# Recurrent mixer on one core: another order of each engine's work, joins over filled rows, weights loaded one stage earlier

## The chip, the core and the metric

The kernel runs on one core of a Trainium2 chip. A core has five engines that run their own instruction streams and meet at semaphores: TensorE (PE in the profile; its weight loads are PEld), VectorE (DVE), ScalarE (ACT), GpSimd (POOL) and SyncE (SP), whose queue here issues nearly all DMAs. The metric is the device time of one execution in microseconds, the median of several runs.

## The reference

A model of two layers over 32 samples of 114 tokens with 256 features each. The change touches the first layer's attention, a gated delta-rule recurrence, cut here to its core:

```python
mixed = hidden_states @ W_qkv.T                 # 2048 channels
y = conv_general_dilated(mixed.T, conv_w, ...)  # 4 taps, one channel each
q, k, v = split(silu(y).T, ...)                 # 8 heads of q, k; 16 of v; 64 wide
z = hidden_states @ W_z.T
beta = sigmoid(hidden_states @ W_b.T)
g = -exp(A_log) * softplus(hidden_states @ W_a.T + dt_bias)
def step(S, (q_t, k_t, v_t, g_t, b_t)):
    S = S * exp(g_t)
    delta = (v_t - k_t @ S) * b_t
    S = S + k_t[:, None] * delta[None, :]
    return S, q_t @ S
o = scan(step, 0, ...)
h = o * silu(z);  h = h * rsqrt(mean(h * h) + EPS) * norm_weight
return h @ W_out.T
```

The rest (image and text embedding, a text layer ahead of it; a mixture of experts, a state-space mixer and a last feed-forward layer behind it) is the same before and after.

## The kernel before

The kernel is a row of stages. Two matter here: `prepare` (lines 837 to 993) and `delta_net` (line 1019 on), which calls it and then runs the mixer.

`prepare` takes the samples in 8 groups of 4: a group is loaded (L864), normalised on VectorE with a power on GpSimd, turned on TensorE (L973), copied by ScalarE (L954) and stored to `xts` (L881); TensorE also makes the gates' products (L983), which VectorE reads into `gates`. SyncE's queue issues the loads and stores; ScalarE's copy of group g waits for the store of group g - 2.

`delta_net` solves the recurrence for 16 pairs of samples. For a pair it computes the projections (`project`, L1601) into `raw`, the conv (`first_tap` on ScalarE, three further taps in `conv` on VectorE, L1322), SiLU by a tanh; the decays exp(sum of g) (`decays` L1589 on TensorE, `decay_terms` and `decay_exp` on ScalarE); the products of keys with keys and queries (`products`); from them `nt`, the weights of the triangular system (L1287, VectorE), and `qd`, the masked queries with decay (`query_decay`, L1187, GpSimd). The system of 114 unknowns for 16 heads and 2 samples is solved through the inverses of its 32 x 32 diagonal blocks: `nt` goes to memory by blocks (L1108), comes back as `ue` with one block in each of the 128 partitions (L1152), is masked on GpSimd (`mask_blocks`, L1206) and inverted by 30 elimination steps of two instructions on VectorE (`eliminate`, L1248 and L1250). The inverses go to memory as they are (`ut` comes back from there, L1139) and turned (`turn_inverse` L1260; they come back into `x`, L1133). Then, for four chains (2 samples, 2 halves of the heads): `join` (L1665) and `inverse` (L1678) make two inverses of 32 into one of 64, `solve` substitutes in two halves (L1700) with a carry between them (L1690) and makes the outputs (L1707). They are multiplied by the gate (`gated`, L1335), normalised, turned and multiplied by `w_out` (L1634).

The work is a software pipeline written out by hand. One call of `iteration(p)` on each engine is one turn: the a-part (decays, products, weights) of pair p, the z-part (elimination, gate, joins, substitution) of pair p - 1, the d-part (norm, output, residual) of pair p - 2 and the projection and conv of pair p + 1. The order of the calls in `iteration` is the order of that engine's stream; nothing else sets it. Five first turns, ten turns in a loop of two, four last turns.

The joins multiply over all 114 rows: the rows of `x` between the blocks must be zero, for which GpSimd clears `x` (`clear_x`, L1196; SyncE waits for it) and VectorE clears a gap after the joins (L1272). The mixer's weights are loaded at its start on SyncE's queue (L1166), VectorE scales `taps` and `w_z` and makes `qmask`, and all engines wait for that.

Of the kernel before, what the change touches and what calls it, by code (L numbers as in the profile page):

```python
# [836 lines left out]
def prepare(c, hid, xts, gates):  # L837
# [5 lines left out]
    with ExitStack() as ctx:  # L843
        def sb(name, shape, dt=F32):
# [9 lines left out]
        (gw_in, gvar_ready, grstd_ready, gxn_ready, g_t, gxT_ready, ab_mm, ab_read, abs_done, log1p_done, g_dve, g_act) = (  # L854
            c.sem(n) for n in ("gw_in", "gvar_ready", "grstd_ready", "gxn_ready", "g_t", "gxT_ready", "ab_mm",
                               "ab_read", "abs_done", "log1p_done", "g_dve", "g_act"))
        h_in = [c.sem(f"g_h_in{n}") for n in range(HB)]
        xT_out = [c.sem(f"g_xT_out{n}") for n in range(2)]
        with nc.Block() as block:

            @block.sync
            def _(sp):
                def load(g):
                    sp.dma_start(hs[g % HB][:, :, :], hid[g * GS:(g + 1) * GS].rearrange("b s d -> s b d")).then_inc(h_in[g % HB], 16)  # L864

# [10 lines left out]
                for g in range(GROUPS):  # L876
                    if g + HB < GROUPS:
                        sp.wait_ge(gxn_ready, g + 1)
                        load(g + HB)
                    sp.wait_ge(gxT_ready, g + 1)  # L880
                    sp.dma_start(xts[:, :, g * L:(g + 1) * L], xT[g % 2][:, :, :]).then_inc(xT_out[g % 2], 16)  # L881
                for n in range(2):
                    sp.wait_ge(xT_out[n], 16 * (GROUPS // 2))

# [7 lines left out]
            def _(dve):  # L892
# [24 lines left out]
                def gate_read(g):  # L917
                    ab = ps[0:S, 4 + g % 2, 0:GS * 2 * H].rearrange("p (s h) -> p s h", s=GS)
# [6 lines left out]
                dve.wait_ge(gw_in, 64)  # L925
                for g in range(GROUPS):
                    if g + 1 < GROUPS:
                        stat(g + 1)
                    scale(g)
                    if g >= 2:  # L930
                        gate_read(g - 2)
                gate_read(GROUPS - 2)
                gate_read(GROUPS - 1)

                dve.wait_ge(ab_read, 2 * GROUPS)
# [28 lines left out]
            def _(pe):  # L964
                pe.wait_ge(gw_in, 64)

# [10 lines left out]
                def gate(g):  # L977
                    pe.wait_ge(gxT_ready, g + 1)
# [36 lines left out]
def delta_net(c, hid, xts):  # L1015
# [14 lines left out]
    with ExitStack() as ctx:  # L1030
        def sb(name, shape, dt=F32):
# [3 lines left out]
        c.stage(prepare, hid, xts, gates)  # L1035
        w_qkv, w_z, w_out = sb("w_qkv", [128, KD, 2048]), sb("w_z", [128, KD, 1024]), sb("w_out", [128, 8, D])
        taps, gain, qmask = sb("taps", [128, CT, TAPS]), sb("gain", [128, 1]), sb("qmask", [S, S])
        xT, xz = sb("d_xT", [128, KD, W]), sb("d_xz", [128, KD, W])
# [14 lines left out]
        (dw_in, d_init, xT_in, xz_in, nd_zero, nd_out, ue_in, ud_out, ut_in, qkv_mm, raw_r, tap_r, conv_r, th_r, yy_r,  # L1053
         kq_mm, qm_r, gl_r, dec_mm, e_r, nt_r, qd_r, sel_r, elim_r, z_mm, thz_r, sz_r, vt_mm, p_mm, rc_r, t_mm, xc_r,
         o_mm, og_r, osq_r, ms_r, rms_r, on_r, ot_mm, oT_r, wo_mm, h_r, d_dve, pe_gate, pool_gate, sp_gate, x_clear,
         uet_r, vd_out, u_in, zz_mm, zs_r, ww_mm, wr_r, x_gap) = (
            c.sem("d_" + s) for s in (
                "w_in", "init", "xT_in", "xz_in", "blocks_zeroed", "blocks_out", "blocks_in", "inverse_out", "inverse_in",
# [3 lines left out]
                "ms_ready", "rms_ready", "on_ready", "ot_mm", "oT_ready", "wo_mm", "h_ready", "dve", "pe_gate", "pool_gate", "sp_gate", "x_cleared",  # L1062
                "inverse_turned", "turned_out", "turned_in", "join1_mm", "join1_ready", "join2_mm", "join2_ready", "x_gap_cleared"))
        h_in = [c.sem(f"d_h_in{s}") for s in range(2)]
        h_out = [c.sem(f"d_h_out{s}") for s in range(2)]
        DW = 7
# [20 lines left out]
        with nc.Block() as block:  # L1087

            @block.sync
            def _(sp):  # L1090
# [19 lines left out]
                def iteration(p, a=True, proj=True, z=True, d=True):  # L1110
# [10 lines left out]
                    if z:  # L1121
# [7 lines left out]
                        sp.wait_ge(x_clear, r.n * 2 + 2)  # L1129
# [23 lines left out]

                sp.dma_start(nd.rearrange("s h q j i -> (s h q) (j i)").rearrange("p (a d) -> p a d", d=D),
                             c.zero_row[:, :].unsqueeze(1).to_broadcast([128, 4, D])).then_inc(nd_zero, 16)
                load_x(Pair(0, 0))
                for dst, src in (
                    (w_qkv[:, :, :], dr["L0_attn_W_qkv_t"].rearrange("(k p) n -> p k n", p=128)),
                    (taps[:, :, :], dr["L0_attn_conv_w_c"]),
                    (w_z[:, :, :], dr["L0_attn_W_z_t"].rearrange("(k p) n -> p k n", p=128)),  # L1160
                    (gain[0:DH, :], dr["L0_attn_norm_weight"].unsqueeze(1)),
                    (gain[DH:128, :], dr["L0_attn_norm_weight"].unsqueeze(1)),
                    (w_out[:, 0:4, :], dr["L0_attn_W_out_t"].rearrange("(k p) n -> p k n", p=128)[:, 0:4, :]),
                    (w_out[:, 4:8, :], dr["L0_attn_W_out_t"].rearrange("(k p) n -> p k n", p=128)[:, 4:8, :]),
                ):
                    sp.dma_start(dst, src).then_inc(dw_in, 16)  # L1166
# [11 lines left out]
            def _(pool):  # L1178
# [13 lines left out]
                def clear_x(r, s):  # L1192

                    need(pool, o_mm, r.n * 4 - 2 + 2 * s)
                    pool.sem_inc(pool_gate, 1)
                    pool.memset(x[s][:, :, :], 0.0).then_inc(x_clear, 1)  # L1196

# [15 lines left out]
                def iteration(p, a=True, proj=True, z=True, d=True):  # L1213
                    r = p.shift(-2)
                    for v in range(4):
                        if a:
                            query_decay(p, 2 * v)
                            query_decay(p, 2 * v + 1)
                        if d and v == 0:
                            gate_power(r, 0)  # L1220
                            gate_power(r, 1)
                        if z and v == 0:
                            clear_x(p.shift(-1), 0)
                            clear_x(p.shift(-1), 1)
                    if a:
# [1790 lines left out]
```

## Time and profile before

| what | value |
|---|---|
| median of 3 runs | 3087.56 us (3084.33 to 3089.98) |
| profiled execution | 3085.63 us |
| its span, first to last instruction | 3083.9 us |
| mean granted TensorE clock | 0.881 |

How to read the page: busy time of each engine, then the span in 40 slices of 77.1 us with the busy share of each slice in tenths (9 is 90% or more).

```profile
PE 2436.0 (79%) x19286; PEld 1864.6 (60%) x19286; DVE 2084.8 (68%) x5004; ACT 1244.2 (40%) x2990; POOL 815.8 (26%) x644
## 2 busy tenths in 40 slices
PE   7888887997458888888888888876452847889698
PEld 5666665886446666666666666655341735566454
DVE  4777774333368888888888888855563336876663
ACT  1334342221256566666666666642000213344132
POOL 2111100001033232232222333221377036450110
PEclk9999998997579999999999999988665877899799
```

`prepare` runs from 739 to 802 us, the mixer from there to about 2165 us: slices 11 to 27. PEclk is the clock that TensorE was granted, in tenths of full speed.

### The profile page before, as it was taken

How to read it: one execution, taken by the hardware profiler on the slowest of the kernel's cores; microseconds unless marked ns; L12 is line 12 of the kernel's file. 1: busy time of each engine (PE TensorE's matmuls, PEld its weight loads, DVE VectorE, ACT ScalarE, POOL GpSimd, SP SyncE). 2: the span in 40 equal slices, each digit the busy share in tenths (PEclk: the TensorE clock that was granted, in tenths of full speed). 3: DMA queues.
4: the chain of work that ended last, by engine and by line, in shares of the span. 5: the costliest groups of instructions: out<-in, count | busy, mean ns of one | idle time of the engine just before them, and what ended most of it. 6: DMA issues, size and time to landing. Idle time of an engine off the chain costs nothing. (4 is left out here: it accounts for less than half of the span.)

```text
span 3083.9 us, 53608 instructions
## 1 busy us (share of the span) xinstructions
PE 2436.0 (79%) x19286; PEld 1864.6 (60%) x19286; DVE 2084.8 (68%) x5004; ACT 1244.2 (40%) x2990; POOL 815.8 (26%) x644
## 2 busy tenths in 40 slices
PE   7888887997458888888888888876452847889698
PEld 5666665886446666666666666655341735566454
DVE  4777774333368888888888888855563336876663
ACT  1334342221256566666666666642000213344132
POOL 2111100001033232232222333221377036450110
PEclk9999998997579999999999999988665877899799
DMA  4210001002201111211122211111211852110000
GB/s 141 72 62 27 12 9 45 21 27 75 100 19 46 49 49 49 50 49 50 49 50 49 50 49 49 46 46 30 88 45 21 263 176 63 45 51 4 18 25 25
DMA packets 274346, 169.01 MB, mean 55 GB/s; under 512 B 182847, under 2 KB 250318, under 8 KB 273728
## 3 DMA queue, kind: packets, MB, share of 16 engines
q1 hardware_dynamic: 247949, 140.28, 15.9%
q0 software_dynamic: 26112, 25.03, 3.1%
q8 instruction: 166, 2.72, 0.4%
q14 instruction: 119, 0.97, 0.1%
HBM read 99.23 MB, written 73.45 MB: 56 GB/s over the span
## 5 line engine op out<-in xcount | busy, mean ns | idle before, releaser
L1187 POOL TENSOR_TENSOR qd<-decay,qm 114x456 f32<-114x456 f32 x128 | 143.4, 1141 | 638.3 <-DVE qm L1280 492.5
L1601 PE MATMUL d_ps<-d_xT,w_qkv 128*128 128x228 f32 x1024 | 236.8, 391 | 44.7 <-DVE qmask L1395 29.2
L1601 PEld LDWEIGHTS d_ps<-d_xT,w_qkv 128*128 128x128 f32 x1024 | 217.2, 213 | 77.1 <-issue 43.2
L2256 POOL DMA_INDIRECT s_eo<-rows_y,slots_all x128 | 152.4, 1191 | 148.3 <-POOLq L87 110.3
L1248 DVE TENSOR_TENSOR elim_tmp<-ue 128x30 f32<-128x30 f32 (+14 forms) x480 | 178.8, 372 | 13.8
L1250 DVE TENSOR_TENSOR ue<-ue,elim_tmp 128x30 f32<-128x30 f32 (+14 forms) x480 | 171.9, 358 | 16.5
L475 PE MATMUL t_ps<-xT,w_qk 128*128 128x154 f32 x1024 | 151.1, 300 | 40.3 <-DVE qk L308 30.9
L1589 PE MATMUL d_ps<-gl,after 114*114 114x456 f32 x256 | 137.2, 654 | 47.2 <-DVE sz L1335 47.2
L1322 DVE SCALAR_TENSOR_TENSOR y_v<-raw,taps,y_v 128x228 f32<-128x228 f32 x384 | 167.1, 508 | 10.6 <-ACT y_v L1452 10.5
L475 PEld LDWEIGHTS t_ps<-xT,w_qk 128*128 128x128 f32 x1024 | 136.7, 189 | 51.8 <-DVE qk L308 38.1
L1206 POOL TENSOR_SCALAR_AFFINE_SELECT ue<-ue 128x1024 f32<-128x1024 f32 x16 | 98.6, 6162 | 238.1 <-DMA ue<-blocks_n 238.1
L1414 ACT ACTIVATE decay<-d_ps,gates 114x114 f32<-114x114 f32 x512 | 133.1, 372 | 64.9 <-PE d_ps L1589 64.5
L1847 POOL DMA_INDIRECT rows_x<-r_xn,slot x128 | 144.3, 1128 | 51.1 <-issue 36.7
L1322 DVE SCALAR_TENSOR_TENSOR y_qk<-raw,taps,y_qk 128x228 f32<-128x228 f32 x384 | 142.2, 450 | 22.0 <-ACT y_qk L1452 21.6
L1425 ACT ACTIVATE gl<-upto,gates 114x114 f32<-114x114 f32 x512 | 151.6, 416 | 0.0
L1634 PE MATMUL d_ps<-w_out,oT 128*114 128x256 f32 x512 | 126.9, 404 | 16.3 <-ACT oT L1471 16.3
L1700 PE MATMUL d_ps<-upd,ut 114*50 114x64 f32 (+1 forms) x2048 | 130.5, 227 | 2.9 <-issue 2.4
L1700 PEld LDWEIGHTS d_ps<-upd,ut 114*50 114x50 f32 (+1 forms) x2048 | 126.5, 138 | 6.2 <-issue 5.7
L1617 PE MATMUL d_ps<-w_z,d_xz 128*114 128x512 f32 x256 | 121.4, 619 | 10.7 <-DVE sz L1311 9.6
L1634 PEld LDWEIGHTS d_ps<-w_out,oT 128*114 128x114 f32 x512 | 95.9, 190 | 46.5 <-ACT oT L1471 20.6
L276 POOL TENSOR_TENSOR rstd<-rstd,minus_half 77x1 f32<-77x1 f32 x32 | 23.4, 732 | 377.2 <-DVE rstd L291 377.2
L415 ACT COPY pT<-t_ps 77x462 f32<-77x462 f32 (+1 forms) x96 | 44.8, 498 | 191.2 <-PE t_ps L525 186.5
(343 smaller groups left out, 5625.0 us busy)
## 6 DMA issues: line engine op xcount, KB each, us to landing
rows_x<-zero_row SPq DMA_DIRECT2D x4, 2048.0 KB, 7.7
ue<-blocks_n SPq DMA_DIRECT2D x16, 512.0 KB, 4.9
blocks_u<-ue SPq DMA_DIRECT2D x16, 512.0 KB, 2.6
blocks_v<-on SPq DMA_DIRECT2D x16, 512.0 KB, 2.7
e_x<-rows_x SPq DMA_DIRECT2D x32, 256.0 KB, 4.3
e_gu<-L_ffn_w_gate_up SPq DMA_DIRECT2D x32, 256.0 KB, 4.3
rows_y<-e_y SPq DMA_DIRECT2D x32, 256.0 KB, 3.4
blocks_n<-nt SPq DMA_DIRECT2D x96, 64.0 KB
```

What stands on the lines that cost most here:

```text
L475: last = pe.matmul(ps[:, 6 + f % 3 % 2, (t - lo) * P2:(t - lo + 1) * P2], w_qk[:, k, t * 128:(t + 1) * 128], xT[pair % 3][:, k, :], start= ...
L1187: pool.tensor_tensor(qd[p.par][s][:, hs(u), :].rearrange("p (a o b) t -> p a o b t", o=2, b=2)[:, :, o], e[o][:, :, :].rearrange("p (a b) ...
L1248: ch(dve.tensor_tensor(part, ue[:, j, j + 1:].unsqueeze(1).to_broadcast([128, j, BW - 1 - j]), ue[:, 0:j, j:j + 1].to_broadcast([128, j, B ...
L1250: step = dve.tensor_tensor(ue[:, 0:j, j + 1:], ue[:, 0:j, j + 1:], part, ALU.subtract)
L1322: dve.scalar_tensor_tensor(y, raw[:, t, :, k:k + S], taps[:, t, k:k + 1], y, ALU.mult, ALU.add).then_inc(conv_r, 1)
L1425: last = act.activation(gl[o][:, m, :], c.upto[:, :], ACT.Copy, scale=gates[:, bass.ds(p.sample(s), 1), head:head + 1].rearrange("p a h -> ...
L1589: pe.matmul(ps[0:S, 4 + o, 0:4 * S].rearrange("p (h t) -> p h t", h=4), c.after[:, :], gl[o][:, :, :], start=True, stop=True).then_inc(dec ...
L1601: last = pe.matmul(ps[:, f % 2, (t % 2) * W:(t % 2 + 1) * W], w_qkv[:, k, t * 128:(t + 1) * 128], xT[:, k, :], start=(k == 0), stop=(k == ...
L1634: last = pe.matmul(ps[0:S, 6, 0:D], oT[:, k, :], w_out[:, k, :], start=(k == 0), stop=(k == 7))
L1700: last = pe.matmul(ps[rows, XBANK[m], i * DH:(i + 1) * DH], ut[s][:, 8 * g + i, rows], x[s][:, 8 * g + i, :], start=True, stop=True)
L1847: pool.indirect_dma_start(out=rows_x, out_offset=bass.IndirectOffsetOnAxis(ap=slot[g % 3][:, s, k:k + 1], axis=0), in_=xn[g % 3][:, s, :], ...
L2256: pool.indirect_dma_start(out=eo[n % EO][:, s * TOPK + k, :], out_offset=None, in_=rows_y, in_offset=bass.IndirectOffsetOnAxis(ap=slots_al ...
```

## The change

Three parts. The diff is cut to its core: where a list of turns is long, the new order is given and the old one is in the kernel above.

Weights. `prepare` gets the mixer's weight tiles and issues their seven loads on SyncE's queue behind the load of the last group; VectorE scales them there, ahead of its wait for `abs_done`. The mixer waits for nothing but the first memset and its own `xT`, whose load is now issued ahead of the zeroing of `blocks_n`. The waits for the gates' weights move behind the first group, and the statistics of group 1 behind the scaling of group 0.

```diff
+                    if g + HB == GROUPS - 1:
+                        load_mixer()
                     sp.wait_ge(gxT_ready, g + 1)
...
+                sp.wait_ge(mix_in, 112)
...
+                ch.note(dve.tensor_scalar(qmask[:, :], c.upto[:, :], -DH ** -0.5, None, ALU.mult))
+                dve.wait_ge(mix_in, 112)
+                ch.note(dve.tensor_scalar(taps[:, :, :], taps[:, :, :], 0.5, None, ALU.mult))
+                ch(dve.tensor_scalar(w_z[:, :, :], w_z[:, :, :], 0.5, None, ALU.mult))
                 dve.wait_ge(ab_read, 2 * GROUPS)
                 dve.wait_ge(abs_done, 1)
...
+                load_x(Pair(0, 0))
                 sp.dma_start(nd.rearrange("s h q j i -> (s h q) (j i)").rearrange("p (a d) -> p a d", d=D),
                              c.zero_row[:, :].unsqueeze(1).to_broadcast([128, 4, D])).then_inc(nd_zero, 16)
-                load_x(Pair(0, 0))
...
-                pe.wait_ge(dw_in, 16 * DW)
-                pe.wait_ge(d_init, INIT + 1)
```

Joins. A join reads only the 32 filled rows of one block; each chain has a first part (rows 0 to 31) and a second (rows 64 to 95), which waits for the chain's first part. The first substitution and the carry read rows 0 to 63. Both clearings of `x` go; SyncE waits for `o_mm` of earlier turns instead of `x_clear`.

```diff
+                def join_part(r, m, n):
+                    s, g = CHAINS[m]
+                    lower, rows, o = JOINS[n]
+                    for i in range(8):
+                        last = pe.matmul(ps[rows, XBANK[m], i * BW:(i + 1) * BW], nt[r.par][s][lower, 8 * g + i, rows],
+                                         x[s][lower, 8 * g + i, o:o + BW], start=True, stop=True)
+                    last.then_inc(zz_mm if n else za_mm, 1)
...
+                    known = HALVES[0] if q == 0 else slice(0, S)
...
+                        last = pe.matmul(ps[rows, XBANK[m], i * DH:(i + 1) * DH], ut[s][known, 8 * g + i, rows],
+                                         x[s][known, 8 * g + i, :], start=True, stop=True)
...
-                    for s in range(2):
-                        rows, _, o = JOINS[1]
-                        dve.memset(x[s][rows, :, o:o + BW], 0.0).then_inc(x_gap, 1)
...
-                        sp.wait_ge(x_clear, r.n * 2 + 2)
+                        need(sp, o_mm, r.n * 4)
```

Order. The helpers are cut smaller (one decay, one tap of a conv group, one chain) and every engine but SyncE gets a new order within the turn. GpSimd and VectorE:

```diff
+                    if d:
+                        gate_power(done, 0)
+                        gate_power(done, 1)
+                    if a:
+                        query_decay(p, 0)
...
+                        query_decay(p, 5)
                         mask_blocks(p)
+                        query_decay(p, 6)
+                        query_decay(p, 7)
```

VectorE, in short (E m-n are elimination steps, qm the query mask, w the weights of one decay, mean, scale and residual those of pair p - 2, silu z the gate's, conv n.k tap k of conv group n):

```
E 1, mean 0, E 2-3, mean 1, E 4-6, scale 0, qm 0, E 7, w 0, E 8, scale 1, E 9-10, w 1, E 11-15, qm 1,
E 16, w 2, w 3, E 17-18, residual 0, E 19, qm 2, E 20-21, w 4, E 22-28, w 5, residual 1, E 29-30,
turned copy, silu z 0, w 6, qm 3, conv 0.1, silu z 1, w 7, conv 0.2, silu z 2, conv 0.3, silu z 3,
join reads 0-3, conv 1.1-3.3, silu 0, gated 0, silu 1, gated 1-3
```

TensorE, in short:

```
decay 0, project 0-1, decay 1, products 0, decay 2, project 2-3, turn 0, decay 3-4, project 4-5,
products 1, project 6, decay 5, output 0, products 2, gate product 0, turn 1, decay 6, output 1,
project 7, decay 7, products 3, values 0, gate products 1-3, join first 0-2, join second 0-1,
join first 3, join second 2, values 1-2, join second 3, values 3, inverse 0-3, substitute 0-3,
carry 0-3, substitute' 0-2, outputs 0, substitute' 3, outputs 1-3
```

ScalarE's order is mixed in the same way: for one, `decay_exp` and `decay_terms` alternate one decay at a time with the reads of the projections, `rhs_read(0, 0)` stands ahead of `first_tap(1)`, and `tanh(1)` ahead of the last `x_read`.

## Rows read from the trace of the kernel before

**Rows 1.** The stretches view: 13 turns. Us, busy us and instructions by engine, clock, DMA.

```profile
1024.86:2040.90 1016.04, 871.79 (x9101) 683.84 (x9100) 884.94 (x1938) 626.20 (x1610) 308.56 (x182) 0.93 0.20 48
```

**Rows 2.** The waits view of VectorE, the same 13 turns.

```profile
DVE join L1268 <- PE d_ps L1665: 23.8, 13, 3.0
DVE nt L1287 <- ACT decay L1414: 21.5, 39, 1.0
DVE sz L1311 <- ACT sz L1465: 17.2, 26, 1.0
DVE y_v L1329 <- ACT raw L1458: 14.0, 13, 1.1
DVE y_v L1322 <- ACT y_v L1452: 10.5, 9, 5.0
DVE qm L1280 <- DVE ue L1250: 6.1, 30, 0.3
```

**Rows 3.** The grouped lines, the same 13 turns (busy us, mean ns | idle before).

```profile
L1700 PE MATMUL d_ps<-upd,ut 114*64 114x64 f32 (+1 forms) x1664 | 105.8, 227 | 1.7 <-issue 1.6
...
L1665 PE MATMUL d_ps<-upd,nt 114*18 114x32 f32 (+1 forms) x1664 | 28.6, 195 | 4.7 <-DMA upd<-blocks_v 4.7
...
L1272 DVE MEMSET upd<- 32x512 f32 x26 | 12.6, 485 | 2.8 <-issue 2.1
```

**Rows 4.** In order of time: GpSimd and VectorE, 1238 to 1253 us.

```profile
1238.92 2.75 POOL L1187 TENSOR_TENSOR qd<-decay,qm 114x456 f32<-114x456 f32 x2
...
1239.47 1.27 DVE L1248 TENSOR_TENSOR elim_tmp<-ue 128x234 f32<-128x234 f32 x1
1240.78 1.16 DVE L1250 TENSOR_TENSOR ue<-ue,elim_tmp 128x234 f32<-128x234 f32 x1
1241.97 0.41 DVE L1248 TENSOR_TENSOR elim_tmp<-ue 128x238 f32<-128x238 f32 x1
...
1252.01 0.94 DVE L1248 TENSOR_TENSOR elim_tmp<-ue 128x220 f32<-128x220 f32 x1
```

**Rows 5.** In order of time: SyncE's queue, TensorE, VectorE, 1261 to 1302 us.

```profile
1261.24 0.34 SPq L1126 DMA_DIRECT2D blocks_v<-on  x1
...
1269.12 2.18 PE L1665 MATMUL d_ps<-upd,nt 114*32 114x32 f32 x128 [1.01 <-DMA upd<-blocks_v]
1274.12 3.30 PE L1678 MATMUL d_ps<-ut,join 114*32 114x32 f32 x128 [2.82 <-DMA ut<-blocks_u]
...
1288.48 6.61 PE L1707 MATMUL d_ps<-upd,qd 114*114 114x64 f32 x64
...
1274.68 8.89 DVE L1322 SCALAR_TENSOR_TENSOR y_qk<-raw,taps,y_qk 128x228 f32<-128x228 f32 x24
...
1300.10 1.87 DVE L1335 TENSOR_TENSOR sz<-sz,d_ps 114x512 f32<-114x512 f32 x3
```

**Rows 6.** One line's instructions: the block mask's first select.

```profile
L1206 POOL TENSOR_SCALAR_AFFINE_SELECT ue<-ue x16: 1271/3482/13424, 896.8 to 2061.9; 128x1024 f32<-128x1024 f32 x16
```

**Rows 7.** In order of time, 765 to 822 us; then issues to landing (KB, us).

```profile
765.41 0.28 SPq L864 DMA_DIRECT2D g_h<-hid  x1
...
776.90 0.92 ACT L954 COPY g_xT<-g_ps 128x912 f32<-128x912 f32 x1 [3.61 <-PE g_ps L973]
...
781.19 3.16 PE L983 MATMUL g_ps<-w_ab,g_xT 128*114 128x32 f32 x16
...
803.22 0.62 SPq L1094 DMA_DIRECT2D d_xT<-normed_t  x1
...
819.37 0.20 DVE L1393 TENSOR_SCALAR taps<-taps 128x64 f32<-128x64 f32 x1 [18.94 <-DMA w_out<-L_attn_W_out_t]
...
821.18 1.10 PE L1601 MATMUL d_ps<-d_xT,w_qkv 128*128 128x228 f32 x2 [29.21 <-DVE qmask L1395]
...
d_xT<-normed_t SPq DMA_DIRECT2D x1, 228.0 KB, 3.8
taps<-L_attn_conv_w_c SPq DMA_DIRECT2D x1, 32.0 KB, 7.7
```

## What the change does to the time: the prediction

> **What bounds the kernel now.** I read the page first, for the stage that the change touches: the mixer runs from 821 to about 2165 us of the 3083.9 us span, most of it in equal turns. The view of one long stretch comes next [rows 1]: 13 turns, from one copy of the turned inverse to the thirteenth after it, take 1016.04 us, so 78.16 us a turn. VectorE is busy 884.94 / 13 = 68.1 us of it, TensorE 871.79 / 13 = 67.1 us, ScalarE 48.2, GpSimd 23.7. Neither of the first two is full: each waits for the other. Then the waits of VectorE in the same stretch [rows 2]: the six longest kinds add up to 93.1 us, 7.16 us a turn; what is left of its 10.1 idle us is small waits and the gaps of some 0.04 us between instructions, and an order can't take the gaps away. So a turn is a VectorE stream of about 71 us with 7.2 us of waits, and a better order can win hardly more than those. Last, the tail of one turn in time [rows 5]: from the turned inverse's store (1261.24) it takes 7.9 us until the first join product (1269.12) and 12.9 us until the second (1274.12, which waits for the DMA), then a chain on TensorE and ScalarE until the outputs end at 1288.48 + 6.61 = 1295.09.
>
> **The order inside a turn.** Per turn, by difference from 78.16.
> - *Waits removed or kept.* The six waits, each against what now stands ahead of it. Join products, 23.8 / 13 = 1.83 us: the first join read stays 7.9 us of DMA plus the products behind the turned inverse. New order: four gate products' SiLU, two kinds of unit work and all of the first conv group (12 instructions, half of the 8.89 us of 24 [rows 5], 4.45 us) stand in between, about 8.6 us; the products are there after 7.9 + 1.7 to 2.2 + 0.25 = 10.1 us, so 1.5 us stay. Decay (21.5 / 13 = 1.65): the exponentials are issued earlier than the weights that read them, 0 stays. Gate tanh (17.2 / 13 = 1.32): a conv chunk of 1.5 us lies in each gap, 0. The SiLU after tanh (14.0 / 13 = 1.08): conv 3 now ends before silu 0, whose 2 us cover the tanh, 0. First tap (0.81): 0. The 0.47 us ahead of the query mask stays. With 0.7 us for new small waits at the turn's end and at the loop's branch, 2.7 us of 7.16 stay: -4.5 us.
> - *Work removed.* The two memsets of the gap: (12.6 + 2.8) / 13 = 1.18 us of VectorE and its gap [rows 3]. -1.2 us. GpSimd's clearing of x goes too (1.8 us), but GpSimd idles over half of the turn: its wait on SP becomes one that was met long before. Nothing.
> - *GpSimd beside VectorE.* This one works against the change. While two query decays run on GpSimd (1238.92 for 2.75 us), two elimination steps take 1.27 and 1.16 us instead of 0.41 [rows 4]: 1.6 us lost; the next pair costs a step 0.94 us instead of 0.39, so 2.15 us a turn now. The other two pairs fall beside instructions that don't suffer. In the new order seven of the eight decays can fall beside an elimination step or the SiLU: decay 0 and 1 at steps 7 and 8 (1.3 us), 2 at step 16 (1.05), 4 and 5 at steps 20 to 22 (2.1); 4.5 us. +2.3 us; between 0 (if as many fall well as now) and +5 us (if each costs its 1.1 us and the two late ones another 0.5).
> - *Joins.* 64 products a turn: 28.6 us / 832 = 34 ns each now, with two places of the array in turn [rows 3]. The new order gives eight in a row to one place. The nearest row for products that follow each other in one place is the substitution: 105.8 / 832 = 127 ns for 64 columns [rows 3], so about 53 to 64 ns at 32. The joins then take 3.4 us instead of 2.2; with three of the four value transposes (1.6 us) behind them they fill the 12.9 - 7.9 = 5.0 us until the inverse's DMA lands. From below they cost what they do now; from above, if load and product no longer overlap at all (twice 53 ns), 6.8 us and +3.4 us a turn. I take +0.1, since the DMA covers it. The substitution's and the carry's products keep their columns and lose only rows; no row shows what that brings, and I take 0, between the same two bounds.
> - *Sum:* -4.5 - 1.2 + 2.3 + 0.1 = -3.3 us. A second way: from the turned copy VectorE needs 8.6 + 1.5 + 3.4 (join reads) + 14.35 (conv 1 to 3) + 6.35 = 34.2 us to the end of the turn, TensorE 12.9 + 20.97 (inverse to outputs, [rows 5]) + 0.9 = 34.8, where the trace has 40.7 us from 1261.24 to the end of the last gated product (1300.10 + 1.87, [rows 5]); minus 5.9, plus 1.5 that the first part grows (the decays' 2.3 less small waits): -4.4. The two chains then tie, so a gain in one alone is worth nothing. I take the middle, -3.8 us: 74.4 us a turn. 14 such turns: -53 us. The short turns at either end have no such overlap to win: 0 (from -4 to +3).
>
> **Weights loaded during prepare.** The mixer's first product starts at 821.18 us, behind three VectorE instructions that waited 18.94 us for w_out's landing [rows 7]. Now it needs only xT: issued at 803.22, 3.8 us to landing; moved ahead of the zeroing it is issued at 802.6, so it starts at 806.8: -14.4 us. Against it: the seven loads (4 MB) are issued behind the last group load at 765.41, on the same queue as the stores of the turned groups, and the small taps load behind the 2 MB one took 7.7 us to land [rows 7], so a queue keeps its order. The weights need 819.2 - 803.9 = 15.3 us, the next store lands near 783 instead of 774. ScalarE's copy of group 5 (776.90) waits for it, 6 us late; TensorE's gate products (3.16 us each) have about 3 us of slack there: +3.5 us. Scaling taps and w_z on VectorE stands ahead of the wait for ScalarE (1.65 us of which 1.2 are covered): +0.5. Of the waits moved behind the first group nothing is won, since the group loads land later. Sum -10.4 us (between -14.4 and -6, if the store's whole delay counts).
>
> **Sum:** 3085.63 (the profiled execution, 1.7 us over its span; the median of the runs is 3087.56, 0.06% more) - 53 - 10.4 = 3022 us.
>
> **The rivals.**
> - *The order finds nearly all of it.* The decays cost no more than now and the joins are free: -4.5 - 1.2 and 0.3 us of small waits, -6.0 us a turn, 3085.6 - 84 - 14 = 2987 us. For it: the two chains above tie at 34 us even with the costs in. Against: seven decays beside two-input instructions.
> - *Only the start is won.* A wait takes the place of the ones removed: ScalarE's turns are now finely mixed, and one late item holds the queue (the first tap of group 1 stands behind the first right-hand-side read, which needs the join). Joins at 6.8 us, or one such wait of 3 to 4 us a turn: 78 us a turn, 3085.6 - 10.4 - 3 = 3072 us.
> - *Slower: small tiles don't overlap.* If each product in a 32 x 32 place waits for the one before it to leave the array, it costs its latency, 195 ns [rows 3]: 64 x 0.195 = 12.5 us, the inverse starts 9.1 us later and the turn is 83.5 us: +5.3 x 14 - 10.4 = +64 us, 3150 us. It decides from 130 ns a join product, where the turn passes 79.3 us. Against: substitutions in one place run at 127 ns with a latency of 227 [rows 3], so products in one place do follow each other inside the array.
> - *Slower by the mask.* The last two decays stand behind the block mask on GpSimd, and ScalarE's first exponential of the next turn behind them. The mask's first select takes from 1.27 to 13.42 us [rows 6]; it starts about 19.5 us after the turned copy, so at 10.2 us it ends, with its second select and one decay, 32.5 us after it, 2 us before the turn's end; only one over 13 us would be felt. It is priced at 0.5 us a turn in the range, and alone reaches slower only over 17 us.
>
> The Trainium skill, page "TensorEngine Tiling (Array Packing)", section "Key Properties", says that changing the tiling mode drains the engine. By it the new order pays about six more drains a turn (the transposes between join halves, the outputs between substitutions). No row of this trace shows such a drain. Taken at the 195 ns of a join product's latency [rows 3], they would be 1.2 us a turn and 17 us in all: 3039 us. That is a rival of its own, inside my range.
>
> **How the numbers follow.** Chances: forecast 0.52 (own range 2998 to 3048), with the drains 0.10, all of it 0.17, only the start 0.13, slower by small tiles 0.06, by the mask 0.02. A measurement of this kernel can tell 0.2%, some 6 us, from no change. Faster: 0.52 + 0.10 + 0.17 + most of 0.13, which lies 0.5% under = 0.88; same 0.04; slower 0.08. The range reaches to the two cases beside the forecast: 2980 to 3068.
>
> **What would show it.** Turn of 74 us between the turned copies; VectorE's waits under 3 us a turn, the one for the join products at 1.5; elimination steps of over 1 us beside seven decays instead of three; 53 to 64 ns a join product; the first mixer product at most 7 us behind the last gates instruction; prepare 4 us longer with ScalarE's copy of group 5 waiting for a store. Wrong if the turn is 78 us with a new wait of TensorE or ScalarE, if join products take over 100 ns, or if the mask moves into the next turn.

## The result

The changed kernel takes 3068.09 us (median; 3041.77 to 3095.43) beside 3086.93 us for the kernel before on the same chips: a ratio of 0.9944 (95% interval 0.992 to 0.9968). That is a gain of some 19 us where the prediction had 63 (3085.63 to 3022). The profiled execution took 3057.6 us, with a span of 3055.8 us and a mean granted clock of 0.876, beside 0.881 before.

From the page of the changed kernel, to be set beside the one ahead of the prediction:

```profile
PE 2497.6 (82%) x19286; PEld 1923.0 (63%) x19286; DVE 2101.1 (69%) x4972; ACT 1246.3 (41%) x2990; POOL 778.4 (25%) x612
## 2 busy tenths in 40 slices
PE   7888887997658999998999999887552847889698
PEclk9999998998678999999999999877665877899799
```

TensorE runs the same 19286 products and is busy 61.6 us longer. This is the first sign of where the gain went: the products got slower, and there are no more of them.

The stretches view shows 13 turns from one turned copy to the thirteenth after it, and then the last turn, which is shorter (columns as in [rows 1]):

```profile
1008.97:2001.02 992.05, 901.55 (x9089) 712.43 (x9088) 901.65 (x1911) 625.13 (x1600) 282.34 (x156) 0.93 0.20 49
2001.02:2074.59 73.57, 61.49 (x600) 50.54 (x599) 36.81 (x89) 19.05 (x35) 10.49 (x6) 0.70 0.18 45
```

A turn takes 992.05 / 13 = 76.3 us instead of 78.16 [rows 1]; 74.4 was forecast. Against the forecast's 3022 us the profiled execution is 35.6 us longer: 25.2 us in fourteen turns (76.2 instead of 74.4), 5.1 in the last one (73.57 us instead of 68.45 before), 6.7 behind it, less 1.5 at the start, whose first turned copy comes 11.85 us earlier (934.23 instead of 946.08).

VectorE's waits in the 13 turns, answering to [rows 2], and grouped lines, answering to [rows 3]:

```profile
DVE join L1274 <- PE d_ps L1747: 34.7, 30, 2.0
DVE sz L1344 <- PE d_ps L1813: 4.4, 3, 2.6
```

```profile
L1331 DVE SCALAR_TENSOR_TENSOR y_v<-raw,taps,y_v 128x228 f32<-128x228 f32 x312 | 160.0, 588 | 2.7 <-ACT y_v L1503 2.5
L1256 DVE TENSOR_TENSOR ue<-ue,elim_tmp 128x30 f32<-128x30 f32 (+14 forms) x390 | 159.0, 408 | 13.4
L1254 DVE TENSOR_TENSOR elim_tmp<-ue 128x30 f32<-128x30 f32 (+14 forms) x390 | 138.8, 356 | 13.7 <-issue 6.1
...
L1747 PE MATMUL d_ps<-upd,nt 32*32 32x32 f32 (+1 forms) x1664 | 61.6, 204 | 19.8 <-DMA upd<-blocks_v 19.0 <-issue 0.8
```

The waits that the order was to remove are gone or down to 2.5 us in 13 turns, but the one for the join products grew from 23.8 to 34.7 us, and the joins' products keep TensorE busy for 61.6 us (by chance the figure that the whole kernel's TensorE gained) instead of 28.6 [rows 3]. One turn's joins in order of time, to be set beside [rows 5]:

```profile
1323.92 4.84 PE L1747 MATMUL d_ps<-upd,nt 32*32 32x32 f32 x112 [1.74 <-DMA upd<-blocks_v]
1328.69 1.96 PE L1738 MATMUL d_ps<-ident,y_v 128*114 128x128 f32 x8
1330.58 1.04 PE L1747 MATMUL d_ps<-upd,nt 32*18 32x32 f32 x16
1331.54 1.10 PE L1738 MATMUL d_ps<-ident,y_v 128*114 128x128 f32 x4
1332.58 3.27 PE L1778 MATMUL d_ps<-ut,join 114*32 114x32 f32 x128
```

From the first join product to the inverse's first it is 8.66 us here, where the forecast had the DMA's 5.0. The experiments had to tell three things apart: the place-by-place sequence of the joins, the changes of the array's shape between them, and the few rows themselves.

### The profile page after: what moved, and what is told of

The parts are those of the page before. It is cut to its first block and busy times, and to the rows that moved or that the text cites. A ratio compares the mean times of both kernels' runs of the same rounds, so it can differ in the third digit from the quotient of the medians.

```text
span 3055.8 us, 53658 instructions
## 1 busy us (share of the span) xinstructions
PE 2497.6 (82%) x19286; PEld 1923.0 (63%) x19286; DVE 2101.1 (69%) x4972; ACT 1246.3 (41%) x2990; POOL 778.4 (25%) x612
## 5 line engine op out<-in xcount | busy, mean ns | idle before, releaser
L1690 PE MATMUL d_ps<-d_xT,w_qkv 128*128 128x228 f32 x1024 | 224.9, 374 | 25.6 <-DMA d_xT<-normed_t 24.4
L1690 PEld LDWEIGHTS d_ps<-d_xT,w_qkv 128*128 128x128 f32 x1024 | 203.3, 201 | 60.2 <-DMA d_xT<-normed_t 26.0
L1256 DVE TENSOR_TENSOR ue<-ue,elim_tmp 128x30 f32<-128x30 f32 (+14 forms) x480 | 194.3, 405 | 16.5
L1465 ACT ACTIVATE decay<-d_ps,gates 114x114 f32<-114x114 f32 x512 | 140.1, 362 | 150.8 <-DVE nt L1296 67.8
L1211 POOL TENSOR_SCALAR_AFFINE_SELECT ue<-ue 128x1024 f32<-128x1024 f32 x16 | 86.5, 5406 | 443.7 <-DMA ue<-blocks_n 443.7
L1331 DVE SCALAR_TENSOR_TENSOR y_v<-raw,taps,y_v 128x228 f32<-128x228 f32 x384 | 190.2, 571 | 2.8 <-ACT y_v L1503 2.5
L1254 DVE TENSOR_TENSOR elim_tmp<-ue 128x30 f32<-128x30 f32 (+14 forms) x480 | 171.3, 357 | 18.4 <-issue 6.1
L1205 POOL TENSOR_TENSOR ms<-ms,minus_half 114x16 f32<-114x16 f32 x32 | 93.8, 2947 | 260.4 <-DVE ms L1305 260.4
L1791 PE MATMUL d_ps<-upd,ut 114*50 114x64 f32 (+1 forms) x2048 | 145.7, 233 | 5.1 <-issue 2.6
L1791 PEld LDWEIGHTS d_ps<-upd,ut 114*50 114x50 f32 (+1 forms) x2048 | 136.2, 142 | 10.9 <-issue 6.7
```

What stands on the lines that cost most here:

```text
L1254: ch(dve.tensor_tensor(part, ue[:, j, j + 1:].unsqueeze(1).to_broadcast([128, j, BW - 1 - j]), ue[:, 0:j, j:j + 1].to_broadcast([128, j, B ...
L1256: step = dve.tensor_tensor(ue[:, 0:j, j + 1:], ue[:, 0:j, j + 1:], part, ALU.subtract)
L1331: dve.scalar_tensor_tensor(y, raw[:, t, :, k:k + S], taps[:, t, k:k + 1], y, ALU.mult, ALU.add).then_inc(conv_r, 1)
L1465: last = act.activation(e[o][:, m, :], ps[0:S, 4 + o, m * S:(m + 1) * S], ACT.Exp, bias=gates[:, bass.ds(p.sample(s), 1), head:head + 1].r ...
L1690: last = pe.matmul(ps[:, f % 2, (t % 2) * W:(t % 2 + 1) * W], w_qkv[:, k, t * 128:(t + 1) * 128], xT[:, k, :], start=(k == 0), stop=(k == ...
L1791: last = pe.matmul(ps[rows, XBANK[m], i * DH:(i + 1) * DH], ut[s][known, 8 * g + i, rows], x[s][known, 8 * g + i, :], start=True, stop=True)
```

## The experiments

"The full-row version" below is the changed kernel in which joins, first substitution and carry multiply over all 114 rows as before (so both clearings of `x` are back, and the two places of the array alternate in the joins), with the changed order and weights.

### The parts alone

Three kernels split the change: the kernel before with only the weights moved; the kernel before, order kept, with only the filled rows; and the full-row version. A fourth is the changed kernel with only the first substitution over all rows; its edit, which the full-row version has too:

```diff
-                    known = HALVES[0] if q == 0 else slice(0, S)
+                    known = slice(0, S)
```

Weights alone:

> The kernel before with the weights' part alone. Both theories: the mixer's first product comes 10 us earlier than before (the changed kernel's trace has 811.33 for 821.18), nothing else moves, so -10 us, 3077 us. Rival: the stall of the stores behind the weights (ScalarE waits 12 us in prepare) costs other turns of the gates more than that in this kernel: 0 us, 3087 us.

Measured: 3071.43 us, ratio 0.9968 (0.9949 to 0.9987), 10.5 us by the medians. The forecast's term of 10.4 us stands.

Filled rows alone, in the old order:

> The kernel before, in the old order, with joins, first substitution and carry over the filled rows alone and both clearings of x gone. Theory A (products over few rows bring TensorE's granted clock down and switch the array's shape): the substitutions of the last two turns run at 110 ns a record instead of 58, +12 us there, and some full turns are held up, against -1.2 us a turn for the memsets: 3080 to 3095 us. Theory B (only GpSimd's decays beside VectorE and the new order's waits took the gain): rows cost nothing, -1.2 x 14 = -17 us, 3070 us.

Measured: 3151.01 us, ratio 1.0212 (1.0186 to 1.0238). This part, costed at nothing, costs 69 us, more than either theory gave it. The stretches view of two of its turns, then TensorE in the first of them and, last, in the second:

```profile
1198.20:1282.30 84.10, 77.58 (x706) 64.08 (x704) 65.11 (x147) 48.94 (x125) 19.63 (x12) 0.84 0.18 45
1369.20:1446.59 77.39, 69.66 (x707) 56.14 (x705) 66.85 (x148) 48.40 (x125) 20.14 (x12) 0.93 0.20 49
```

```profile
1221.23 6.71 PE L1686 MATMUL d_ps<-upd,nt 64*50 64x64 f32 x61
1227.87 6.08 PE L1695 MATMUL d_ps<-upd,ut 114*50 114x64 f32 x64
...
1389.73 3.57 PE L1686 MATMUL d_ps<-upd,nt 64*50 64x64 f32 x61
```

The same 706 or 707 TensorE instructions take 84 us at a granted clock of 0.84 and 77 us at 0.93, and the carry takes 6.71 us for 61 records, 110 ns each, at the lower clock; the same 61, over 64 rows as well, take 3.57 us, 59 ns each, at the full clock. The ratio is near that of the clock's two levels, 1.2 and 2.4 GHz. The kernel before falls to the lower level here too, in nine of fifteen turns, 13 to 19 us behind the turned copy, for 3.4 us in all but one. With the few rows it falls in all fifteen, 10 to 14 us behind it, and stays down for 20.5 or 23.9 us in nine of them.

All rows, changed order and weights:

> The changed kernel with joins, substitution and carry over all rows again, both clearings of x back, two places of the array in turn as before. Theory A: the last two turns come back to 58 ns a record (-12 us), the turn loses the join waits of 1.2 us and gains the memsets of 1.2 us: 3055 us where the changed kernel is 3068, and the times scatter less. Theory B: +1.2 us a turn, 3085 us.

Measured: 3011.21 us, ratio 0.9779 (0.9757 to 0.98), 57 us less than the changed kernel by the medians, 51 by the ratios, where the larger of the two expectations had 13. Its stretch of 13 turns:

```profile
1009.03:1972.86 963.83, 843.98 (x9086) 660.66 (x9086) 891.54 (x1937) 625.48 (x1600) 370.68 (x182) 0.97 0.21 51
```

74.14 us a turn: the new order does what was forecast of it, once the rows are out of it.

> The changed kernel with the first substitution alone over all 114 rows (its other rows multiply zeros), joins and carry as changed. Theory A: part of the substitution runs at the full clock again, -3 to -8 us against the changed kernel, 3062 us. Theory B: no difference, 3068 us. If only the joins (32 rows) lower the clock, no difference either.

Measured: 3041.51 us, ratio 0.9872 (0.985 to 0.9894): giving only the first substitution its rows back returns 27 of the 57 us by the medians, 22 of the 51 by the ratios.

### Which products, and is it rows or sequence

Five kernels start from the full-row version and take back one thing each: few rows in substitution and carry together, in the first substitution alone, in the carry alone; the joins place by place, first with all rows, then with their 32 filled rows.

```diff
-                        for _, rows, o in JOINS:
-                            last = pe.matmul(ps[rows, XBANK[m], i * BW:(i + 1) * BW], nt[r.par][s][:, 8 * g + i, rows],
-                                             x[s][:, 8 * g + i, o:o + BW], start=True, stop=True)
+                        last = pe.matmul(ps[rows, XBANK[m], i * BW:(i + 1) * BW], nt[r.par][s][lower, 8 * g + i, rows],
+                                         x[s][lower, 8 * g + i, o:o + BW], start=True, stop=True)
```

(That is the last of the five; with `:` for `lower` it is the fourth.)

> The full-row version of the changed kernel (3011 us), with the first substitution and the carry over the filled 64 rows again; the joins stay over all rows. Theory A1 (the granted clock falls because the substitution and the carry run over few rows): most of the 57 us comes back, 3045 to 3065 us, the clock falls 20 to 30 us behind the turned copy. Theory A2 (it is the joins over 32 rows, by their switches of the array's shape and by running eight in one place, that bring the clock down or hold the turn up): within 8 us of 3011.

Measured: 3081.56 us, ratio 0.9985 (0.9961 to 1.0008), 64 us over the full-row version by the ratios, 70 by the medians.

> The full-row version (ratio 0.9779 to the kernel before) with only the first substitution over its 64 filled rows: 64 of the 128 products a turn that f_subrows shortened (the other 64 are the carry). f_subrows lost 70 us by both. If each product over fewer rows costs the same, this is about +35 us: ratio 0.989. If it is the length of the stretch of few-row products that brings the clock down, the loss is under 15 us: ratio 0.978 to 0.983, and low stretches of the granted clock behind the turned copy are as rare as in the full-row version. If only the first substitution matters, +60 to +70 us.

Measured: 3045.66 us, ratio 0.9888 (0.9856 to 0.9919): +34 us by the ratios.

> The full-row version with only the carry over its 64 filled rows. Equal shares: +35 us, ratio 0.989. If it is the length of the stretch of few-row products: under 15 us. If the carry is what matters: +60 to +70 us, and f_sub shows the full-row version's time.

Measured: 3016.76 us, ratio 0.9791 (0.9759 to 0.9824): +4 us, not to be told from none. Equal shares fall: alone, the first substitution is felt and the carry isn't, and together they cost more than their sum.

> The full-row version with the joins place by place as in the changed kernel (eight products into one place, then, later, eight into the other, transposes between them), still over all rows. It shows what the sequence costs without the few rows. If the sequence alone costs: 53 to 64 ns a product instead of 35, 1.2 us more of TensorE, of which 0.5 to 1 us a turn is felt, 3018 to 3026 us. If the switch between array shapes by rows is what costs, no difference from 3011 us and 53 to 64 ns a product.

Measured: 3030.34 us, ratio 0.9836 (0.9814 to 0.9859): +18 us for the sequence alone.

> The full-row version with the joins of the change: over 32 filled rows, place by place, the second parts behind the wait for the first; substitution and carry over all rows. The same sequence with full rows (f_joinseq) ran at 0.9836. If few rows cost the joins nothing of their own, 0.984. If they bring the clock down as in substitution and carry (32 of 114 rows, but only 64 short products), up to +20 us more: 0.990. If the place changes with few rows (32 x 32 tiles against 128 x 32 ones) drain the array, a turn is 1 to 2 us longer than f_joinseq's 75.0 at a full clock: 0.988 to 0.993. The changed kernel lost 57 us against the full-row version; what f_sub, f_carry and this one don't account for is an interaction.

Measured: 3052.0 us, ratio 0.9904 (0.987 to 0.9938): 21 us more for the same sequence over 32 rows. One wait is added here too, for each chain's first join part; the next fences show that it takes nothing at the full clock. First the joins of the fourth kernel (all rows, place by place), then of the fifth (filled rows) in one of its turns, then of the fifth in another, in order of time:

```profile
1316.61 3.27 PE L1759 MATMUL d_ps<-upd,nt 114*32 114x32 f32 x112 [2.11 <-DMA upd<-blocks_v]
1319.82 1.09 PE L1750 MATMUL d_ps<-ident,y_v 128*114 128x128 f32 x8
1320.83 0.64 PE L1759 MATMUL d_ps<-upd,nt 114*18 114x32 f32 x16
1321.41 0.65 PE L1750 MATMUL d_ps<-ident,y_v 128*114 128x128 f32 x4
1321.98 2.21 PE L1789 MATMUL d_ps<-ut,join 114*32 114x32 f32 x128
```

```profile
1330.66 3.27 PE L1759 MATMUL d_ps<-upd,nt 32*32 32x32 f32 x112 [0.62 <-DMA upd<-blocks_v]
1333.86 1.09 PE L1750 MATMUL d_ps<-ident,y_v 128*114 128x128 f32 x8
1334.88 0.64 PE L1759 MATMUL d_ps<-upd,nt 32*18 32x32 f32 x16
```

```profile
1255.72 1.96 PE L1750 MATMUL d_ps<-ident,y_v 128*114 128x128 f32 x8
1257.61 1.04 PE L1759 MATMUL d_ps<-upd,nt 32*18 32x32 f32 x16
```

At the full clock few rows and all rows take the same time to a hundredth: 3.27, 1.09, 0.64 us (and the carry 3.57 us over 64 rows in the old order, as over 114 in the fifth kernel). So neither the rows nor the shape of the tile costs a product anything by itself. In the turn at 1255 the same groups take 1.96 and 1.04 us. The stretches view of that turn and the one behind it, both of the fifth kernel:

```profile
1240.95:1322.85 81.90, 74.40 (x708) 59.12 (x704) 71.06 (x150) 48.43 (x124) 19.71 (x14) 0.88 0.19 47
1322.85:1396.19 73.34, 66.83 (x710) 52.72 (x707) 68.75 (x149) 48.38 (x125) 29.92 (x14) 0.98 0.21 51
```

One turn has the clock, 73.34 us; its neighbour loses 8.56 us. The records of the granted clock put the half-clock stretches where the few-row products run: in this kernel 6.8 to 13.7 us, beginning 7.7 to 12.4 us behind the turned copy (with the joins), in twelve of fifteen turns; in the one with only the first substitution short, 3.4 to 10.2 us, beginning 16.8 to 19.7 us behind it, in nine; with the carry short as well, 10.2 to 20.5 us, beginning 14.5 to 21.4 us behind it, in eleven; in the changed kernel 6.8 to 27.3 us, beginning 9.5 to 19.0 us behind it, in all fifteen. In the full-row version two of fifteen turns have one that begins between 7 and 22 us, of 3.4 us each, both after some 2 us of idle time of TensorE.

What TensorE did before the clock fell differs. In the turn at 1240.95 it fell with the first join product, after a wait of 2.09 us for the DMA, so the few rows didn't bring it down there; it then stayed down for 13.7 us. In another turn of the fifth kernel it fell after 3.77 us of join products over 32 rows and transposes with no pause, behind a wait of 1.48 us (the stretches view, from the first join product to the fall, and the lower level):

```profile
1867.70:1871.47 3.77, 3.77 (x117) 3.72 (x118) 2.67 (x7) 1.65 (x5) 0.00 (x0) 1.00 0.75 116
1871.48:1878.29 6.81, 6.81 (x157) 5.99 (x156) 5.63 (x15) 4.62 (x14) 0.00 (x0) 0.50 0.51 111
```

In the fourth kernel, the same sequence over all rows, it fell at this place in one of fifteen turns, for 3.4 us.

The last solve, where TensorE has nothing else to mix in, shows what a stay at the lower level costs. Stretches of 524 records each, from the first join product to the last output: first the changed kernel, and in it the stretch at the lower level:

```profile
2082.44:2121.49 39.05, 39.05 (x524) 37.64 (x524) 5.45 (x11) 12.66 (x25) 0.00 (x0) 0.61 0.10 20
2082.71:2113.42 30.71, 30.71 (x438) 29.66 (x435) 3.38 (x8) 10.45 (x22) 0.00 (x0) 0.50 0.12 24
```

Then the full-row version, and below it the first of the five kernels, with substitution and carry over 64 rows:

```profile
2043.49:2069.59 26.10, 23.70 (x524) 22.93 (x524) 6.42 (x13) 12.67 (x25) 0.00 (x0) 1.00 0.15 30
```

```profile
2108.50:2134.57 26.07, 23.83 (x524) 22.97 (x524) 6.43 (x13) 12.68 (x25) 0.00 (x0) 1.00 0.15 30
```

The changed kernel is busy all the time, 39.05 us at a clock of 0.61; the full-row version waits for ScalarE and DMA in between, and still ends after 26.10 us. The wait ahead of the first join is much the same in both (2.48 and 2.42 us for the DMA). In the changed kernel the clock fell 0.27 us behind the first join product, so early that the few rows can hardly have brought it down; why it fell here and not in the full-row version, this pair doesn't show. What it does show is that the clock stayed at 1.2 GHz for 30.7 us while TensorE never paused. And where it didn't fall, few rows cost nothing: the solve with substitution and carry over 64 rows takes 26.07 us. So the price of the few rows isn't paid in every turn. The clock falls in more turns, and once it's down it stays down longer.

The Trainium skill, page "TensorE: Matmul & The Clock Gate", says in "Step-by-step: what each phase is for" that the time of a weight load goes by its columns and that the row count doesn't matter. The fences show load and product together, and at the full clock they agree: 3.27 us over 32 rows and over 114. In "What's actually happening" it has the clock depend on how busy TensorE has been, and names no rows; with TensorE busy for all of 30.71 us at 0.50, the trace differs, and the measurement decides.

### GpSimd beside VectorE

From the full-row version, the query decays write one column of 114; the others are cleared once, at the start. It leaves out the rest of the decayed queries, so that most outputs of the mixer lack their term.

```diff
-                        qm[u][:, o, :, :].unsqueeze(2).to_broadcast([S, 2, 2, S]), ALU.mult).then_inc(qd_r, 1)
+                        qm[u][:, o, :, 0:1].unsqueeze(2).to_broadcast([S, 2, 2, 1]), ALU.mult).then_inc(qd_r, 1)
```

> The full-row version with the eight query decays on GpSimd cut to one column each (part of the outputs is left out, so this is a price, not a version). If their port use beside VectorE's two-input instructions costs what the prediction took (4.5 us a turn, now 3.4 us by the longer elimination and conv steps): -3.4 x 14 = -48 us, 2963 us, as far as TensorE does not become the bound; TensorE's chain ties, so -1.5 us a turn, 2990 us, is the other end. If it costs nothing, 3011 us.

Measured: 2959.61 us, ratio 0.9601 (0.9577 to 0.9625), 52 us less than the full-row version, 3.7 us a turn. The grouped lines over 13 turns, first of the full-row version (elimination and conv of `y_v`), then of this kernel (elimination; its conv is unchanged at 117.8 us):

```profile
L1265 DVE TENSOR_TENSOR ue<-ue,elim_tmp 128x30 f32<-128x30 f32 (+14 forms) x390 | 159.9, 410 | 13.4
L1263 DVE TENSOR_TENSOR elim_tmp<-ue 128x30 f32<-128x30 f32 (+14 forms) x390 | 146.0, 374 | 17.3 <-issue 9.7
...
L1340 DVE SCALAR_TENSOR_TENSOR y_v<-raw,taps,y_v 128x228 f32<-128x228 f32 x312 | 117.9, 458 | 1.7 <-ACT y_v L1515 1.7
```

```profile
L1267 DVE TENSOR_TENSOR ue<-ue,elim_tmp 128x30 f32<-128x30 f32 (+14 forms) x390 | 130.2, 334 | 13.4
L1265 DVE TENSOR_TENSOR elim_tmp<-ue 128x30 f32<-128x30 f32 (+14 forms) x390 | 128.2, 329 | 17.5 <-issue 9.9
```

The elimination gives back (159.9 + 146.0 - 130.2 - 128.2) / 13 = 3.65 us a turn, and the turn is 3.50 us shorter in the traces (70.64 instead of 74.14): it's the whole gain.

### Where the start's stall comes from

In the changed kernel SyncE issues the weights from 762.31 to 774.44 us; ScalarE's copy of group 5 and the mixer's first product follow, in order of time:

```profile
785.88 0.92 ACT L976 COPY g_xT<-g_ps 128x912 f32<-128x912 f32 x1 [16.03 <-DMA normed_t<-g_xT]
...
811.33 1.89 PE L1690 MATMUL d_ps<-d_xT,w_qkv 128*128 128x228 f32 x4 [13.55 <-DMA d_xT<-normed_t]
```

Two kernels from the full-row version: the weights issued from ScalarE's queue at group 4; and, on SyncE's, in quarters of about 1 MB, one behind each of the stores of groups 3 to 6.

```diff
-                    if g + HB == GROUPS - 1:
-                        load_mixer()
...
+                    if 3 <= g < 7:
+                        for dst, src in PARTS[g - 3]:
+                            sp.dma_start(dst, src).then_inc(mix_in, 16)
```

> The full-row version with the mixer's seven weight loads issued from ScalarE's queue in prepare instead of SyncE's. If the stores stood behind the weights because a queue keeps its order, ScalarE's copy of group 5 no longer waits 16 us and prepare ends 5 us earlier: 3006 us. If the DMA engines themselves were full, the stores wait all the same: 3011 us.

Measured: 3017.52 us, ratio 0.979 (0.9769 to 0.9811): the same as the full-row version. The copy still waits for the store (9.96 us, since the copy of group 4 came 5.4 us later than in the full-row version):

```profile
785.93 0.92 ACT L976 COPY g_xT<-g_ps 128x912 f32<-128x912 f32 x1 [9.96 <-DMA normed_t<-g_xT]
```

> The full-row version with the mixer's weights issued on SyncE's queue in four parts of about 1 MB, one behind each store of a turned group (groups 3 to 6), in place of all 4 MB ahead of them. In the full-row version ScalarE's copy of group 5 waited 16.0 us for a store; moving the loads to another queue left that wait (it was then 10.0 us behind a late load), so the 16 DMA engines serve them in the order of issue whatever the queue. If that is right the copies of groups 5 to 7 start within 2 us of their old rhythm (one in 4.5 us) and the gates end 6 to 10 us earlier: 3002 to 3006 us on that chip, ratio 0.975. If the engines share among whatever is pending, the stores are slowed as much as before and the time stays at 0.978. Slower (0.980) only if the last weights land after the gates are ready.

Measured: 3001.3 us, ratio 0.9744 (0.9715 to 0.9774). The last copies of its `prepare`:

```profile
774.36 0.92 ACT L977 COPY g_xT<-g_ps 128x912 f32<-128x912 f32 x1 [3.92 <-DMA normed_t<-g_xT]
780.67 0.92 ACT L977 COPY g_xT<-g_ps 128x912 f32<-128x912 f32 x1 [5.38 <-DMA normed_t<-g_xT]
784.57 0.92 ACT L977 COPY g_xT<-g_ps 128x912 f32<-128x912 f32 x1 [2.99 <-PE g_ps L994]
```

The 16 us wait is 5.38 us. From the copy of group 1 to that of group 7 it is 28.96 us instead of 36.40 in the full-row version, 7.4 us less, as expected; in this execution group 1 came 4.1 us later, so the first turned copy is only 4.5 us earlier (930.32 against 934.78). Its interval overlaps that of the full-row version, and its profiled execution was a long one (3015.99 us; the full-row version's took 3010.23), so its gain of 10 us over that one isn't shown by the times; the trace shows the shorter `prepare`. Against both kernels it is clearly faster: 2.6% under the kernel before, and 62 us under the changed one by the ratios. Here the store waited for the loads issued ahead of it from either queue, and what shortened its wait was to issue less ahead of it. The Trainium skill, page "DMA: Bandwidth & Descriptors", section "Issuing engines are not separate DMA queues", says that transfers started by ScalarE, SyncE or GpSimd run on the same 16 DMA engines; the two copies at 785.9 us agree.

## Why the prediction was right or wrong

The range missed by a tenth of a us (3068.09 against 3068), the gain by much more: 19 us instead of 63, for the most part in one step. That the range nearly held is luck: its upper end stood for a late wait in every turn, and what came was a lower clock.

- **What bounds the kernel, the waits in the order:** right. Without the few rows the turn is 74.14 us, 74.4 forecast. The full-row version still has the memsets (1.2 us), so its order gains 4.0 us where the prediction's terms would leave 2.6. VectorE's idle time fell from 10.08 to 5.56 us a turn, the 4.5 us of the waits' term, though not wait by wait (the one for the join products was to keep 1.5 us and kept 3.0 / 13 = 0.2); its busy time rose by 0.5 us, where 2.3 was forecast.
- **The failed step: "The substitution's and the carry's products keep their columns and lose only rows; no row shows what that brings, and I take 0".** The term was bounded like the joins, by load and product not overlapping (at most +3.4 us a turn, 48 us), and its value taken at the lower end. In the old order the few rows of joins, substitution and carry cost 69 us, in the new one those of substitution and carry alone 64, and the whole part 57 together with the joins' sequence. The price isn't in the products but in the clock, which holds for all that TensorE does just then (the transposes too: 1.96 us instead of 1.09). The bounds were drawn from durations at the full clock and couldn't hold it. The prediction had the clock's column in [rows 1] (0.93, with TensorE busy 86% of the time) and gave it no term: a turn's price at the other of the clock's levels was the bound that was missing.
- **Joins, +0.1 us:** the size of one product was right: 3.21 us for 56 products is 57 ns, 53 to 64 forecast. The cover was not enough. From the first join product to the inverse it takes 5.37 us in the place-by-place version (1316.61 to 1321.98), against 4.88 us with the DMA as the last in the full-row version, and the first join read is later too; 18 us in all instead of 1.4. VectorE's wait there, forecast at 1.5 us a turn, was 17.0 / 13 = 1.3 in the place-by-place version over all rows, but 34.7 / 13 = 2.7 in the changed kernel. What the forecast left out is that few rows cost the joins another 21 us by the clock.
- **Drains on a change of shape:** 3039 us was given for 195 ns each. Between 1319.82 and 1321.98 us twelve transposes (1.52 us in the full-row version's one run) and 16 join records (0.46 us at 29 ns) leave under 0.2 us for three changes: less than 0.1 us each, and the same with 32 rows. Such a drain may well exist; its price is small here.
- **GpSimd beside VectorE, +2.3 us:** the changed kernel's elimination and `y_v` conv take (159.0 + 138.8 + 160.0) against (139.0 + 147.4 + 136.3) us before, +2.7 us a turn. But 1.8 of it is the conv, which the prediction didn't name: in the turn at 1315 the last two decays (1344.27 for 2.37 us) run beside it. In the full-row version the same sum is +0.1 us. The term was the right size for partly another reason.
- **Rival "only the start is won", 3072 us:** nearest to the time. It had the joins or a new wait at 3 to 4 us a turn. In fact, beside the full-row version's trace, fourteen turns lost 28.7 us, the last turn 10.7 (73.57 instead of 62.83) and what lies behind it 8.4, by the clock and the joins' sequence. Right in size, for another reason.
- **Slower by small tiles:** false as told, products in one 32 x 32 place follow at 57 ns, not 195. **The mask:** its first select takes 5.4 us in the median of 13 turns, and the last two decays behind it end 31 us behind the turned copy in the turn at 1315, far from the next turn.
- **Weights, -10.4 us:** measured -10.5. The stall was larger than forecast (ScalarE waits 16.0 us ahead of group 5, where it waited 3.6 [rows 7] and 6 more were forecast), but group 6 followed at once, and the gates end 5.8 us later instead of 4. The prediction laid the stall to the order kept within one queue; the loads issued from ScalarE's queue held the store up too.

What stays open: why products over fewer rows are granted the lower clock, and why the effects don't add (34 and 4 us apart, 64 together, and 51 with the joins and their sequence and without the clearings, all by the ratios). The runs show that the clock falls in more turns and for longer, and where, but not by what rule. Nor is the difference between the changed kernel and the full-row version clock alone: the joins' sequence costs 18 us by itself.

## What to carry to other kernels

Zero rows in a product were free here and leaving them out was dear. Where TensorE helps to set the time, compare the granted clock of the stretch before and after any edit that makes products smaller, even if each product's own duration can't change. When a change has several parts, the one costed at nothing without a row is the one to build alone first. A load issued early can hold up the stores behind it: 16 us here behind 4 MB, 5.4 us with the loads in quarters between the stores.

## What was not expected of the hardware

TensorE, busy for 39.05 us without a gap, was granted 0.61 of its clock when joins, first substitution and carry covered 32 and 64 rows, and 1.00 in 26.10 us with pauses when they covered 114. With full rows the same 13 turns ran at 0.97, with few at 0.93 in the changed kernel and 0.91 with only substitution and carry short. Few rows don't lower it every time: the last solve with substitution and carry over 64 rows ran at 1.00. One place of the array takes 57 ns a join product of 32 columns at the full clock, over 32 rows as over 114; two places in turn take 33 ns (over 114 rows).
